# Own probabilities of two batches side by side: one 128x128 transpose for two heads, turns and weighings moved by a step

## The chip, the cores and the metric

The kernel runs on one core of a Trainium2 chip. The metric is the time of one execution on the device in microseconds (us). The engines are TensorE (PE, with its weight loads PEld), VectorE (DVE), ScalarE (ACT), GpSimd (POOL) and SyncE (SP, which only issues DMAs here). They run side by side, each in its own order, and wait for each other on semaphores.

## The reference

One decoder layer on x of shape 8 x 64 x 256 (batch, query, width) with a context of 8 x 1601 x 256, in fp32:

```python
x = x + xattn(layernorm(x), ctx, ctx)      # 16 heads of 16; keys and values from the 1601 rows of the context
x = x + attn(layernorm(x), causal=True)    # own attention: 16 heads, 64 queries x 64 keys in each batch
x = x + moe(layernorm(x))                  # 8 experts 256 -> 1024 -> 256, the best 2 by a softmax router
```

The change concerns the own attention: scores q k / 4 under a causal mask, softmax over the 64 keys, and the weighted sum of the values.

## The kernel before

The 512 tokens are four tiles of 128 rows, each two batches of 64 queries. The cross attention is the bulk: `tile(t, units)` runs 26 steps for a tile, 13 (`KT`) blocks of 128 context rows for its first batch (`bi` 0) and 13 for its second. In a step PE adds the shift and computes the scores of the block (lines 1386 and 1400), ACT takes the exponentials (line 743), POOL adds them into `prob_sum` (line 494), and PE weighs the values with them a step later (line 1220). PE begins step n only when the exponentials of step n-1 are done (line 1378); ACT begins those of step n only when POOL's sum of step n-2 is. At the second step of a batch PE computes the denominators of the batch before from `prob_sum` (line 1418 waits for POOL's last sum) and DVE then takes the heads out of the bank (lines 858 and 859).

Other work is woven into these steps as *units*, each filling one PSUM bank: K (keys of the next batch), M (a product whose row maximum DVE takes, line 927), V (values, lines 1211 and 633), X (the shift rows, lines 1260 and 637), and the *chain* of what follows the cross attention for the tile before. `CHAIN_AT` says at which step each piece of the chain runs in tiles 1 and 2, `CHAIN_AT_LAST` in tile 3, and `CHAIN_ALONE` in the tail, where the chain of the last tile runs among the first expert's products. `step_units` puts the units of a step in order (M, K, chain, V), and `Units` gives them banks in rotation: five banks (`RING_BANKS`), from the second half of tile 3 on three (`LATE_BANKS`), in the tail four (`ALONE_BANKS`). A unit waits until the unit that had its bank before has been read (`wait_free`), by ACT if its kind is in `READ_BY_ACT`, else by DVE. All instructions of an engine stand in one order written out by these tables.

The part of the chain that the change touches, in tiles 1 and 2, by step:

- 8 and 10: `s0`, `s1`, own scores of the tile's batch 0 and 1 (line 1324). DVE adds the mask (944), takes the row maxima (845) and subtracts them (846); ACT takes the exponential a step later (674); DVE sums and divides two steps later (851 to 853). The result is `soft`, 128 rows (two heads of 64 queries) by 8 pairs of heads by 64 keys, once for each batch.
- 12: `t00`, `t01`, the transposes of batch 0's probabilities, four pairs of heads in each: PE turns 128 x 64 into 64 x 128 in partitions 0 to 63 of the bank (1334). ACT copies 64 x 512 to `probs2` (652).
- 13: `t10`, `t11`, the same for batch 1 into partitions 64 to 127, as plain fp32 products with the identity (1336), which the trace shows as two passes each.
- 14 and 15: `o0`, `o1`, the values weighed (1343 to 1345); DVE takes each head's part (837, 838). At 17 follows `y2`, the output projection (1349).

In tile 3 these stand at 7, 9, 11, 12 and 14 (`o0` and `o1` together); in the tail at 5, 7 and 8.

## Time and profile before

| | before |
|---|---|
| timed runs (us) | 658.1, 660.2, 660.26; median 660.2 |
| profiled execution (us) | 658.37, its span 656.6 |
| busy: PE, PEld | 628.2 (96%), 530.1 (81%) |
| busy: DVE, ACT, POOL | 472.9 (72%), 329.8 (50%), 305.1 (46%) |
| mean granted clock of TensorE | 0.995 |
| L1334, transposes of batch 0 | 32 of 272 ns |
| L1336, passes for batch 1 | 64 of 275 ns |
| L652, copies to `probs2` | 16 of 590 ns |

The span runs from the first to the last instruction; 1.8 us of the execution lie around it. Busy times of PE overlap: matmuls are pipelined, and what one costs is the distance to the start of the next, not its duration. The main loop's tile 1 runs from about 141 us, tile 2 from about 250, tile 3 from about 359, and the experts' work with the tail's chain begins at about 445.

### The profile page before, as it was taken

The numbers are of one execution on the slowest core, as the hardware profiler recorded it, in microseconds if no ns is written. First come the engines' busy times: TensorE is split into PE (matmuls) and PEld (weight loads), VectorE is DVE, ScalarE is ACT, GpSimd is POOL, SyncE is SP. The second block draws the span as 40 slices with busy tenths as digits, with TensorE's granted clock in tenths as the row PEclk, the third lists the DMA queues.
The fourth block names the chain that finished last, engine by engine and source line by source line (L and its number), as shares of the span: only waits on it lengthen the run. The fifth ranks groups of instructions, "written<-read, shape, count | busy, mean of one in ns | idle before, by whom it ended". The sixth has DMA issues, their size and how long they took to land.

```text
span 656.6 us, 15592 instructions
## 1 busy us (share of the span) xinstructions
PE 628.2 (96%) x6312; PEld 530.1 (81%) x6312; DVE 472.9 (72%) x878; ACT 329.8 (50%) x541; POOL 305.1 (46%) x386
## 2 busy tenths in 40 slices
PE   6989999999989999998999999988989999999997
PEld 4778878868877877887887887767889999999997
DVE  4887767757697687587876867587777667756653
ACT  4355655555555564546465546474554444444421
POOL 2138788898696798687779868200000000000000
PEclk9999999999999999999999999999979999999999
DMA  6312011010010010011100000333003311330000
GB/s 183 137 46 57 27 51 27 27 51 27 27 38 15 27 52 26 26 27 51 27 27 26 2 1 2 128 132 129 1 4 125 129 50 80 128 128 0 0 0 33
DMA packets 13285, 34.11 MB, mean 52 GB/s; under 512 B 1563, under 2 KB 10532, under 8 KB 11044
## 3 DMA queue, kind: packets, MB, share of 16 engines
q1 hardware_dynamic: 13188, 33.19, 15.2%
q8 instruction: 46, 0.75, 0.5%
q14 instruction: 19, 0.16, 0.1%
q0 software_dynamic: 32, 0.01, 0.0%
HBM read 32.67 MB, written 0.52 MB: 51 GB/s over the span
## 4 chain that ended last, share of the span: by engine, by line
PE 69%; DVE 14%; POOL 8%; issue 5%; ACT 2%; DMA 1%; SPq 0%; POOLq 0%; DVEq 0%; ACTq 0%
PE bank L1211 44%; POOL prob_sum L494 8%; PE bank L1400 7%; PE bank L1220 6%; PE bank L1386 3%; PE bank L1281 3%; DVE maxes L927 2%; DVE prob_sum L494 2%; DVE ctx_lo L478 1%; DVE k_lo L908 1%; PE bank L1336 1%; DVE shift L869 1%; ACT k_hi L630 1%; PE bank L1308 1%; DVE qbd L873 1%
## 5 line engine op out<-in xcount | busy, mean ns | idle before, releaser
L494 POOL TENSOR_TENSOR prob_sum<-probs,prob_sum 128x256 f32<-128x256 f32 x336 | 273.9, 846 | 61.6 <-ACT probs L743 56.1
L743 ACT ACTIVATE probs<-bank 128x1024 f32<-128x1024 f32 (+1 forms) x104 | 106.7, 1026 | 110.1 <-PE bank L1400 80.9
L927 DVE TENSOR_REDUCE maxes<-bank 128x1 f32<-128x400 f32 (+1 forms) x256 | 129.4, 564 | 16.5 <-PE bank L1281 16.0
L725 ACT ACTIVATE h_raw<-bank,b_sb 128x512 f32<-128x512 f32 (+2 forms) x72 | 46.2, 642 | 104.9 <-PE bank L1211 101.0
L908 DVE SCALAR_TENSOR_TENSOR k_lo<-bank,bias_sb,k_hi 128x400 fp32r<-128x400 f32 (+2 forms) x64 | 40.4, 631 | 47.6 <-ACT k_hi L630 47.5
L1211 PE MATMUL bank<-w_hi,h_hi 128*128 128x256 f32 x256 | 73.7, 288 | 0.5 <-DVE h_lo L1146 0.5
L1211 PE MATMUL bank<-w_lo,h_hi 128*128 128x256 f32 x256 | 73.1, 286 | 0.0
L1211 PE MATMUL bank<-w_hi,h_lo 128*128 128x256 f32 x256 | 73.1, 285 | 0.0
L1220 PE MATMUL bank<-probs,v_sb 128*32 128x128 f32 (+1 forms) x1664 | 67.0, 279 | 2.0 <-ACT probs L743 1.9
L1145 DVE CAST h_hi<-h_raw 128x512 fp32r<-128x512 f32 (+2 forms) x72 | 28.5, 396 | 55.9 <-ACT h_raw L725 54.5
L1211 PE MATMUL bank<-wv_hi,ctx_hi 128*128 128x256 f32 (+1 forms) x208 | 65.1, 313 | 2.8 <-DVE maxes L927 2.6
L1400 PE MATMUL bank<-qbd_hi,k_hi 64*128 64x256 f32 (+1 forms) x416 | 66.5, 314 | 0.0
L1281 PE MATMUL bank<-k_hi,qbd_hi 64*128 64x400 f32 (+1 forms) x256 | 58.6, 443 | 1.0 <-DVE qbd_hi L885 0.4
L1400 PE MATMUL bank<-qbd_lo,k_hi 64*128 64x256 f32 (+1 forms) x416 | 58.8, 277 | 0.0
L1400 PE MATMUL bank<-qbd_hi,k_lo 64*128 64x256 f32 (+1 forms) x416 | 58.7, 277 | 0.0
L1211 PE MATMUL bank<-wv_lo,ctx_hi 128*128 128x256 f32 (+1 forms) x208 | 58.4, 281 | 0.0
L1211 PE MATMUL bank<-wv_hi,ctx_lo 128*128 128x256 f32 (+1 forms) x208 | 58.1, 279 | 0.0
L633 ACT ACTIVATE v_sb<-bank 128x256 f32<-128x256 f32 (+1 forms) x104 | 39.8, 382 | 35.5 <-PE bank L1211 32.0
L630 ACT ACTIVATE k_hi<-bank,bias_sb 128x400 fp32r<-128x400 f32 (+2 forms) x64 | 38.1, 596 | 38.2 <-PE bank L1211 38.2
L1211 PE MATMUL bank<-xn_hi,w_hi 128*128 128x512 f32 (+2 forms) x144 | 55.1, 382 | 0.0
L1211 PE MATMUL bank<-xn_hi,w_lo 128*128 128x512 f32 (+2 forms) x144 | 54.4, 377 | 0.0
L1211 PE MATMUL bank<-xn_lo,w_hi 128*128 128x512 f32 (+2 forms) x144 | 54.3, 377 | 0.0
(155 smaller groups left out, 1386.7 us busy)
## 6 DMA issues: line engine op xcount, KB each, us to landing
raw<-in_w SPq DMA_DIRECT2D x16, 1024.0 KB, 6.8
ctx_raw<-in_ctx_t SPq DMA_DIRECT2D x16, 400.0 KB, 3.6
ctx_raw<-in_ctx_t SPq DMA_DIRECT2D x8, 402.0 KB, 3.7
ctx_raw<-in_ctx_t SPq DMA_DIRECT2D x8, 399.0 KB, 3.6
w_sb<-in_w_t SPq DMA_DIRECT2D x1, 1280.0 KB
w_raw<-in_w_t SPq DMA_DIRECT2D x2, 256.0 KB, 4.7
result<-x_all SPq DMA_DIRECT2D x4, 128.0 KB, 1.9
x_all<-in_x SPq DMA_DIRECT2D x1, 384.0 KB, 4.1
```

Source lines behind the costliest of these rows:

```text
L494: ins = engine.tensor_tensor(prob_sum[0:ROWS[k], cols], probs[0:ROWS[k], s % 2, cols], acc[0:ROWS[k]], ALU.add)
L630: nc.scalar.activation(k_hi[parity][:, g, EDGE[c]:EDGE[c + 1]], src[:, EDGE[c] - CH[c]:CW], ACT.Identity, bias=bias_sb[:, 1, g:g + 1]).the ...
L633: nc.scalar.activation(v_sb[0:ROWS[u], u * D:u * D + D], src[0:ROWS[u], 0:D], ACT.Copy).then_inc(read_act, 1)
L725: nc.scalar.activation(h_raw[:, c % 2, 0:width], bank[:, at, 0:width], ACT.Gelu, bias=b1_sb[:, bass.ds(e, 1), c:c + 1].rearrange("p a b -> ...
L743: nc.scalar.activation(probs[0:ROWS[k], s % 2, :].rearrange("p (g n) -> p g n", g=G), bank[0:ROWS[k], score_bank(b, k):score_bank(b, k) + ...
L908: nc.vector.scalar_tensor_tensor(out=k_lo[parity][:, g, EDGE[c]:EDGE[c + 1]], in0=src[:, EDGE[c] - CH[c]:CW], scalar=bias_sb[:, 1, g:g + 1 ...
L927: nc.vector.tensor_reduce(maxes[:, g * PAIRS + j, c:c + 1], src[:, 0:width], AX.X, ALU.max).then_inc(read_dve, 1)
L1145: link(nc.vector.tensor_copy(h_hi[:, c % 4, 0:width], h_raw[:, c % 2, 0:width]))
L1211: last = nc.tensor.matmul(dst, lhs, rhs, start=(start and n == 1), stop=(stop and n == 3 * len(pairs)), **more)
L1220: ins = nc.tensor.matmul(dst_bank[32 * j:32 * j + 32, (at + g) * P:(at + g + 1) * P], lhs(g, j), p_rows[:, m * P:(m + 1) * P], start=(star ...
L1281: ins = nc.tensor.matmul(dst[:, 0:width], qbd_hi[rows, parity, g, 2 * i:2 * i + 2, :].rearrange("p s q -> p (s q)"), k_hi[parity][rows, g, ...
L1400: ins = nc.tensor.matmul(bank[0:rows, score_bank(b, k) + r, g * RH * Q:(g + 1) * RH * Q], stays, moves, start=False, stop=(part == 2), ski ...
```

## The change

`soft` is laid out with the two batches of a pair of heads side by side, so that one transpose of 128 x 128 turns both: query rows of two heads by 64 keys of batch 0 and 64 keys of batch 1. Four units `t00`, `t01`, `t10`, `t11` become two, `t0` and `t1`, which wait for the division of both batches; the products with the identity are gone. The copies to `probs2` take all 128 partitions. In tiles 1 and 2 the turns stand at step 14 and both weighings at 15; in tile 3 the turns at 13 and the weighings at 14 as before; in the tail the places stay. With two units fewer the banks rotate otherwise, and in the tail `gt` and `b2` get banks by name. DVE and ACT reach a batch's part of `soft` in pieces of 64 with a step of 128.

```diff
--- before.py
+++ after.py
@@ -100,15 +100,15 @@
 OWN_V = {0: 11, 1: 12}
 LAST_V_AT = 1
 
-CHAIN_AT = {3: ["y1"], 5: ["xt1"], 6: ["qk", "v"], 8: ["s0"], 10: ["s1"], 12: ["t00", "t01"], 13: ["t10", "t11"],
-            14: ["o0"], 15: ["o1"], 17: ["y2"], 19: ["xt2"], 20: ["router"], 24: ["gt"], 25: ["b2"]}
-
-CHAIN_AT_LAST = {2: ["y1"], 4: ["xt1"], 5: ["qk", "v"], 7: ["s0"], 9: ["s1"], 11: ["t00", "t01"],
-                 12: ["t10", "t11"], 14: ["o0", "o1"], 16: ["y2"], 18: ["xt2"], 19: ["router"], 23: ["gt"],
-                 24: ["b2"]}
-CHAIN_ALONE = {1: ["y1"], 2: ["xt1"], 3: ["qk"], 5: ["s0", "s1", "v"], 7: ["t00", "t01", "t10", "t11"],
+CHAIN_AT = {3: ["y1"], 5: ["xt1"], 6: ["qk", "v"], 8: ["s0"], 10: ["s1"], 14: ["t0", "t1"],
+            15: ["o0", "o1"], 17: ["y2"], 19: ["xt2"], 20: ["router"], 24: ["gt"], 25: ["b2"]}
+
+CHAIN_AT_LAST = {2: ["y1"], 4: ["xt1"], 5: ["qk", "v"], 7: ["s0"], 9: ["s1"], 13: ["t0", "t1"], 14: ["o0", "o1"],
+                 16: ["y2"], 18: ["xt2"], 19: ["router"], 23: ["gt"], 24: ["b2"]}
+CHAIN_ALONE = {1: ["y1"], 2: ["xt1"], 3: ["qk"], 5: ["s0", "s1", "v"], 7: ["t0", "t1"],
                8: ["o0", "o1"], 9: ["y2"], 11: ["xt2"], 12: ["router"], 15: ["gt"], 16: ["b2"]}
 ALONE_BANKS = [6, 2, 7, 3]
+GATE_BANKS = {"gt": 3, "b2": 6}
 DONE_TILES = TT - 1
 FIRST_HIDDEN = {0: [2], 1: [3], 3: [4], 6: [5], 7: [6], 9: [7]}
 FIRST_GELU = {0: [0, 1], 1: [2], 2: [3], 4: [4], 8: [5, 6], 9: [7]}
@@ -126,7 +126,7 @@
     return [("M", ROW_TILES * u + r) for u in pairs for r in range(ROW_TILES)]
 
 
-READ_BY_ACT = {"p1", "p2", "p3", "v", "V", "VL", "X", "xt1", "qk", "t00", "t01", "t10", "t11", "xt2", "router", "gt"}
+READ_BY_ACT = {"p1", "p2", "p3", "v", "V", "VL", "X", "xt1", "qk", "t0", "t1", "xt2", "router", "gt"}
 
 
 class Units:
@@ -153,6 +153,9 @@
         self.early = sum(len(self.at[s]) for s in range(KT))
         self.bank = [late_banks[n % len(late_banks)] if late_banks and n >= self.early else banks[n % len(banks)]
                      for n in range(len(order))]
+        if banks is ALONE_BANKS:
+            for n, kind in enumerate(order):
+                self.bank[n] = GATE_BANKS.get(kind, self.bank[n])
 
     def counts(self, n):
 
@@ -330,7 +333,7 @@
         own = masked[:, 0:2 * G, :]
         odd = masked[:, 2 * G:4 * G, :]
         neg_max2 = sb("neg_max2", [P, 2, G * PAIRS])
-        soft = sb("soft", [P, 2, G * PAIRS, Q])
+        soft = sb("soft", [P, G * PAIRS, 2, Q])
         row_sums2 = sb("row_sums2", [P, 2, G * PAIRS])
         odd2 = sb("odd2", [P, 2, G, Q])
         probs2 = sb("probs2", [P, G * 512])
@@ -647,10 +650,8 @@
                 elif kind == "v":
                     nc.scalar.activation(v2[:, :], src[:, 0:D], ACT.Copy).then_inc(read_act, 1)
                 elif kind[0] == "t":
-                    bi, g = int(kind[1]), int(kind[2])
-                    rows = slice(bi * Q, bi * Q + Q)
-                    nc.scalar.activation(probs2[rows, g * 512:g * 512 + 512], src[rows, :], ACT.Copy)\
-                        .then_inc(read_act, 1)
+                    g = int(kind[1])
+                    nc.scalar.activation(probs2[:, g * 512:g * 512 + 512], src, ACT.Copy).then_inc(read_act, 1)
                 elif kind == "xt2":
                     nc.scalar.activation(xn_t[:, :, :].rearrange("p c n -> p (c n)"), src[:, 0:D],
                                          ACT.Copy).then_inc(read_act, 1)
@@ -671,7 +672,7 @@
                     if kind in ("s0", "s1"):
                         bi = int(kind[1])
                         act.wait_ge(soft_ready, 2 * t + bi + 1)
-                        nc.scalar.activation(soft[:, bi], soft[:, bi], ACT.Exp).then_inc(soft_exp_done, 1)
+                        nc.scalar.activation(soft[:, :, bi, :], soft[:, :, bi, :], ACT.Exp).then_inc(soft_exp_done, 1)
 
             def step(units, s, t, b, parity):
 
@@ -842,15 +843,15 @@
                 return values.unsqueeze(2).broadcast_to([P, G * PAIRS, Q])
 
             def subtract_maxima(bi):
-                link(nc.vector.tensor_reduce(neg_max2[:, bi], soft[:, bi], AX.X, ALU.max, negate=True))
-                nc.vector.tensor_tensor(soft[:, bi], soft[:, bi], by_row(neg_max2[:, bi]), ALU.add).then_inc(soft_ready, 1)
+                link(nc.vector.tensor_reduce(neg_max2[:, bi], soft[:, :, bi, :], AX.X, ALU.max, negate=True))
+                nc.vector.tensor_tensor(soft[:, :, bi, :], soft[:, :, bi, :], by_row(neg_max2[:, bi]), ALU.add).then_inc(soft_ready, 1)
 
             def divide_rows(bi, count):
 
                 dve.wait_ge(soft_exp_done, count)
-                link(nc.vector.tensor_reduce(row_sums2[:, bi], soft[:, bi], AX.X, ALU.add))
+                link(nc.vector.tensor_reduce(row_sums2[:, bi], soft[:, :, bi, :], AX.X, ALU.add))
                 link(nc.vector.reciprocal(row_sums2[:, bi], row_sums2[:, bi]))
-                nc.vector.tensor_tensor(soft[:, bi], soft[:, bi], by_row(row_sums2[:, bi]), ALU.mult).then_inc(rows2_ready, 1)
+                nc.vector.tensor_tensor(soft[:, :, bi, :], soft[:, :, bi, :], by_row(row_sums2[:, bi]), ALU.mult).then_inc(rows2_ready, 1)
 
             def own_heads(src, read, count):
 
@@ -941,7 +942,7 @@
                                             ALU.add).then_inc(read_dve, 1)
                 elif kind in ("s0", "s1"):
 
-                    nc.vector.tensor_tensor(soft[:, int(kind[1])], src.rearrange("p (n k) -> p n k", k=Q),
+                    nc.vector.tensor_tensor(soft[:, :, int(kind[1]), :], src.rearrange("p (n k) -> p n k", k=Q),
                                             causal_sb[:, :].unsqueeze(1).broadcast_to([P, G * PAIRS, Q]),
                                             ALU.add).then_inc(read_dve, 1)
                 elif kind in ("o0", "o1"):
@@ -1326,19 +1327,16 @@
                                                    k2_t[:, g, bi * Q:bi * Q + Q], start=True, stop=True)
                 elif kind[0] == "t":
 
-                    bi, g = int(kind[1]), int(kind[2])
-                    pe.wait_ge(rows2_ready, 2 * t + bi + 1)
+                    g = int(kind[1])
+                    pe.wait_ge(rows2_ready, 2 * t + 2)
                     for j in range(PAIRS):
-                        turned, own_rows = dst[bi * Q:bi * Q + Q, j * P:j * P + P], soft[:, bi, g * PAIRS + j, :]
-                        if bi == 0:
-                            ins = nc.tensor.transpose(turned, own_rows, ident[:, :])
-                        else:
-                            ins = nc.tensor.matmul(turned, own_rows, ident[:, :], start=True, stop=True)
+                        ins = nc.tensor.transpose(dst[:, j * P:j * P + P],
+                                                  soft[:, g * PAIRS + j].rearrange("p b q -> p (b q)"), ident[:, :])
                 elif kind in ("o0", "o1"):
 
                     bi = int(kind[1])
                     rows = slice(bi * Q, bi * Q + Q)
-                    units.wait_read_act(pe, read_act, f"t{bi}1")
+                    units.wait_read_act(pe, read_act, "t1")
 
                     nc.tensor.matmul(dst[:, 0:E], ones_bf[:, :], ident_bf[:, 0:E], start=True, stop=True)
                     ins = weigh_heads(dst, 0, lambda g, j: v2[rows, g * P + 32 * j:g * P + 32 * j + 32],
```

## Rows read from the trace of the kernel before

**Rows 1.** The page's chain that ended last: share of the span by engine
```profile
PE 69%; DVE 14%; POOL 8%; issue 5%; ACT 2%; DMA 1%; SPq 0%; POOLq 0%; DVEq 0%; ACTq 0%
```

**Rows 2.** Timeline of PE, step 12 of tile 1: start us, duration us, instruction, idle before
```profile
191.35 1.03 PE L1334 MATMUL bank<-ident,soft 128*64 128x128 f32 x8 [1.72 <-DVE soft L853]
192.14 0.36 PE L1211 MATMUL bank<-wv_hi,ctx_hi 128*128 128x256 f32 x1
...
193.59 0.39 PE L1386 MATMUL bank<-shift_rows,ones_bf 64*128 64x512 bf16 x2
```

**Rows 3.** Timeline of ACT in the same stretch
```profile
190.71 1.06 ACT L637 ACTIVATE shift_rows<-bank 128x512 bf16<-128x512 f32 x2
191.67 1.02 ACT L743 ACTIVATE probs<-bank 65x1024 f32<-65x1024 f32 x1
192.57 1.07 ACT L652 ACTIVATE probs<-bank 64x512 f32<-64x512 f32 x2
```

**Rows 4.** Timeline of PE, step 13 of tile 1
```profile
195.91 1.96 PE L1336 MATMUL bank<-ident,soft 128*64 128x128 f32 x16
197.80 0.38 PE L1211 MATMUL bank<-wv_hi,ctx_hi 128*128 128x256 f32 x1
```

**Rows 5.** Timeline of PE, steps 14 and 15 of tile 1: denominators, o0, o1
```profile
200.48 0.64 PE L1220 MATMUL bank<-prob_sum,ones_f 128*32 128x128 f32 x16
...
202.87 0.18 PE L1343 MATMUL bank<-ident_bf,ones_bf 128*128 128x8 bf16 x1
...
207.59 0.18 PE L1343 MATMUL bank<-ident_bf,ones_bf 128*128 128x8 bf16 x1
...
208.27 0.65 PE L1220 MATMUL bank<-probs,v_sb 128*32 128x128 f32 x16
```

**Rows 6.** Timeline of POOL: a sum of tile 1, two sums of tile 3
```profile
192.76 4.58 POOL L494 TENSOR_TENSOR prob_sum<-probs,prob_sum 65x256 f32<-65x256 f32 x4 [0.27 <-ACT probs L743]
...
402.89 6.45 POOL L494 TENSOR_TENSOR prob_sum<-probs,prob_sum 128x256 f32<-128x256 f32 x8 [0.76 <-ACT probs L743]
```

**Rows 7.** Timeline of DVE, step 14 of tile 1
```profile
202.23 2.03 DVE L927 TENSOR_REDUCE maxes<-bank 128x1 f32<-128x402 f32 x4
```

**Rows 8.** Timeline of PE, step 11 of tile 3
```profile
403.96 0.28 PE L1400 MATMUL bank<-qbd_hi,k_lo 64*128 64x256 f32 x2
...
405.80 0.36 PE L1211 MATMUL bank<-wv_hi,ctx_hi 128*128 128x256 f32 x1
```

**Rows 9.** Transposes: ns min/median/max by line, and one pair in PE's timeline
```profile
L1235 PEld LDWEIGHTS bank<-ident,xn x24: 138/140/143, 5.1 to 477.8; 128*128 128x128 f32 x24
L1235 PE MATMUL bank<-ident,xn x24: 271/273/329, 5.2 to 477.9; 128*128 128x128 f32 x24
...
L1334 PEld LDWEIGHTS bank<-ident,soft x32: 108/111/113, 191.3 to 467.4; 128*64 128x64 f32 x32
...
477.74 0.41 PE L1235 MATMUL bank<-ident,xn 128*128 128x128 f32 x2 [0.81 <-DVE xn L830]
```

**Rows 10.** Instructions by line and form: busy us, mean ns | idle before
```profile
L944 DVE TENSOR_TENSOR soft<-bank,causal_sb 128x512 f32<-128x512 f32 x8 | 5.5, 683 | 1.1 <-PE bank L1324 1.0
...
L859 DVE SCALAR_TENSOR_TENSOR masked<-bank,mask_sb,masked 128x256 f32<-128x256 f32 x8 | 3.9, 484 | 0.3
...
L838 DVE SCALAR_TENSOR_TENSOR o_t<-bank,mask_sb,odd 128x128 f32<-128x128 f32 x8 | 2.8, 351 | 0.3
```

**Rows 11.** Timeline of PE in the tail
```profile
468.29 1.93 PE L1336 MATMUL bank<-ident,soft 128*64 128x128 f32 x16 [0.52 <-DVE soft L853]
470.15 0.44 PE L1211 MATMUL bank<-xn_hi,w_hi 128*128 128x384 f32 x1
```

**Rows 12.** Busy time by stretch; the number after POOL's is the granted clock
```profile
478.00:482.00 4.00, 2.94 (x15) 2.70 (x14) 2.95 (x8) 2.29 (x5) 0.00 (x0) 0.64 0.01 2
482.00:486.00 4.00, 4.00 (x22) 4.00 (x20) 1.86 (x9) 1.82 (x5) 0.00 (x0) 0.51 0.00 0
486.00:490.00 4.00, 3.91 (x31) 3.41 (x31) 3.68 (x12) 3.11 (x9) 0.00 (x0) 1.00 0.00 0
```

## The prediction

> **What bounds the kernel now.** I read the chain that ended last first, because it says which engine's time is the kernel's time: 69% of it is TensorE (PE), 14% VectorE (DVE), 8% GpSimd (POOL), 2% ScalarE (ACT) [rows 1]. An instruction taken from PE is therefore worth its time, provided that PE does not meet a wait a moment later that it used to reach late. So the second view is the timeline of PE around every place where the change works. These are four: the chain of own attention runs once for each of four pairs of batches. It is woven into tiles 1, 2 and 3 of the main loop (schedules MIDDLE, MIDDLE, LAST) and once into the first expert's work (TAIL). The steps of tiles 1 and 2 repeat each other within 0.1 us in start-to-start time, so I show tile 1 and count it twice. The third view is the other engines in the same stretches, to see what is late next.
>
> **What the change removes on PE.** Per pair of batches there are now 8 transposes (batch 0, line 1334), issued in 1.03 us, and 16 matmul passes (batch 1, line 1336: 8 fp32 products of two passes each) in 1.96 us [rows 2, 4]. PE's next work starts 0.79 us after the first group (191.35 to 192.14) and 1.89 us after the second (195.91 to 197.80); the first also has a wait of 1.72 us before it, for the division of batch 0's rows by DVE [rows 2, 4]. The change puts 8 transposes of 128 columns in their place. The trace has this very shape in the transposes of the normalised tile (line 1235), but only in pairs: two take 0.41 us, one 0.27, so the second starts 0.14 us behind the first [rows 9]. Of the 64-column ones, with the same last part of 0.27, one follows the other every (1.03 - 0.27)/7 = 0.109 us [rows 2]. Bounds: 8 x 0.109 = 0.87 us and 8 x 0.14 = 1.12 us per pair; I take 1.0, between them, since the first gap of a group tends to be the long one, and a pair has no other.
>
> **Tile 1, step 12** (the next step starts at 193.59 [rows 2]). Gone are the wait and the 8 transposes: 1.72 + 0.79 = 2.5 us of PE's time. It can't use all of it. Step 13 begins with a wait for the exponentials of step 12 (line 1378), and ACT starts these at 191.67 and ends at 192.69, because they stand in its queue behind the exponential of the own scores, a split and the two copies of the shift rows, which end at 191.77 [rows 3]. None of that is touched. PE's other work of the step (V projection and weighing, 192.14 to 193.59) then ends at about 191.1, and step 13 starts at 192.75 instead of 193.59: **0.84 us** gained, and PE now idles in front of the exponentials for 1.6 us where it idled 1.72 us for the division.
>
> **Step 13.** t10 and t11 go: from 195.91 to 197.80, **1.89 us** [rows 4]. The K unit before them and the V unit behind them follow without a wait. Next comes step 14's score work and then the denominators, which wait for POOL's sum of step 12. POOL ends that at 192.76 + 4.58 = 197.34 [rows 6]; the denominators came at 200.48 [rows 5] and will come at about 200.48 - 0.84 - 1.89 = 197.75. Covered, by 0.4 us.
>
> **Step 14.** It loses o0 (0.68 us: the equal o1 starts with line 1343 at 207.59 and the next work at 208.27) and gets t0 and t1 (1.0 us): **+0.3 us** [rows 5]. Before, o0 waited for the bank that DVE's first maximum frees (DVE reads the four from 202.23 on, 0.51 us each [rows 7]); t0 takes over that wait, t1 needs the second maximum at 203.25 and the V unit the third at 203.76, each just when the transposes end. Nothing is added within 0.1 us. The new wait for both batches' rows is over before: in step 13 PE took up batch 1's rows at 195.91 with no wait [rows 4], so nothing queued behind it on PE (t0, t1, the V unit, the next weighing) is held up. In the tail the same wait ends at 468.29 as now; behind it stands the hidden product, which stood there before. **Step 15** gets o0 beside o1: **+0.68**. DVE's reads of o0 move with it, in the same number.
>
> Sum of a middle tile: -0.84 - 1.89 + 0.3 + 0.68 = -1.75; twice, **-3.5 us**. ACT gets two copies of 128x512 for four of 64x512: two of the old ones take 1.07, two copies of a whole 128x512 (the shift rows) 1.06 [rows 3], so it saves 1.07 per pair, which hides behind PE and counts nothing. DVE, ACT's exponential and PE now see `soft` in pieces of 64 with a step of 128. DVE reads of PSUM with such steps: 0.351 us for 128 elements, 0.484 for 256, so 0.133 per 128 and 0.75 for 512, against 0.683 of the present contiguous form [rows 10]. Bounds: 0 and 0.07 per instruction. In the middle tiles at most three of them lie before the exponentials of step 12 (0.2 us); in the tail ten in a row (0.7 us). I take nothing, because 0.484 is no more than the 128-element form plus its elements (two pieces or four cost the same), and keep 1.3 us for the range.
>
> **Tile 3 (LAST).** t00 and t01 stand in step 11: PE's score work starts its last pair at 403.96 and the V unit at 405.80 [rows 8]; without them it starts about 0.2 later than the last score, at 404.2: -1.6. The exponential behind it waits for PE here, not PE for it. Step 12 loses t10 and t11, -1.9 (the same 16 passes as in tile 1 [rows 4]). Step 13 gets t0 and t1, +1.0. o0 stays in step 14. Sum **-2.5 us**; POOL's sums of steps 10 and 11 ended together at 402.89 + 6.45 = 409.34 [rows 6]; step 13's exponentials wait for the second and would now be ready at about 409.8, so this cover too is 0.4 us.
>
> **Tail.** PE waits for batch 1's division until 468.29, turns its rows, and goes on to the next hidden product at 470.15 [rows 11]. The 8 transposes of batch 0, earlier, lie in a hole and count nothing; after the division come now 1.0 us instead of 1.86: **-0.85 us**. What follows (weighings, projection, normalisation, routing) is a chain of latencies and moves up as a whole.
>
> **The sum**: 3.5 + 2.5 + 0.85 = 6.85, say 6.8 us. The profiled execution took 658.4 us (span 656.6 and 1.8 around it), so it would be 651.6. The timed runs stand at 658.1, 660.2 and 660.3: two levels 2 us apart, and the profiled one belongs to the lower. The median by the upper level would be 653.4. I have no reason to expect that the levels vanish, nor which the median will catch, and forecast **652.8**, slightly nearer the upper one since that holds the median now.
>
> On the price of the transposes a rule speaks against the change. The row: a load of 64 columns for a transpose takes 0.110 us and one of 128 columns 0.140, while transposes follow each other at 0.11 and 0.14 us [rows 2, 9]. The Trainium skill, TensorE: Matmul & The Clock Gate, section LDWEIGHTS (loading the stationary operand), says that a load takes time in proportion to its columns, P/1.2 ns. By that page, as an estimate, the 24 loads of 64 columns cost 1.28 us now and the 8 of 128 columns 0.85, and the change would be worth 0.4 us per pair where I count 1.7 to 1.9; the trace's two load times don't double.
>
> **Rivals.**
> 1. *A full-width transpose costs two half-width ones.* Then 8 of them take 8 x 0.22 = 1.75 us, 0.75 more in each of the four places: 3.0 less gain, 655.8. Against it stands the pair at 0.14. Chance 0.06.
> 2. *The wait moves instead of going.* The cover of the denominators in step 14 is 0.4 us. Should POOL's sum end later, or DVE's reads take the place, the 1.89 of step 13 in two tiles is lost: gain 3.1, 657.1 by the upper level, 655.3 by the lower. For it: POOL takes 1.15 us for each of this sum's four pieces and 0.81 for one in tile 3 [rows 6], so its time is not fixed. Against: it starts at the end of the exponentials, which the change leaves. Chance 0.08.
> 3. *The clock.* TensorE's granted clock falls in the tail: 0.64 in 478 to 482 and 0.51 in 482 to 486, which is its 1.2 GHz level, after a stretch in which PE waited much, and is back to 1.00 (2.4 GHz) in 486 to 490. At the low level PE passes 22 matmuls in 4 us, at the high one 31 [rows 12], so the 6.8 us at the low level (the shares below 1.00, doubled) cost 6.8 x 9/31 = 2.0 us. That is also the distance of the two levels of the runs. The tail gets emptier, all of it before 470, so one fall may become longer or two: +2.0, 654.8 to 655.4. Chance 0.12. It may also not fall: 650.8, inside the forecast's range, chance 0.05.
> 4. *Slower than before.* The same mechanism in more places: if the new hole in front of step 12's exponentials brought the clock down in both middle tiles, and the tail had two falls more, each at 2.0 us, the time would be 652.8 + 8.0 = 660.8; with rival 2's loss, 664.5. Falls decide from four on (6.8/2.0 = 3.4), or from two beside rival 2. Against it: the present hole there is as long (1.72 us) and the transposes behind it go at full pace [rows 2]. Chance 0.03.
>
> That the change doesn't do what it says has no way open: the transposes' shape is fixed in the code.
>
> **How the numbers follow.** Forecast 0.66 (and 0.05 for the clock that doesn't fall), with its own range 650.3 to 655.2 (bounds of the transposes -0.5 and +0.5, of the steps +1.3, of the two levels -1.2 and +0.6, of chaining in the steps 0.5). Rival 1 and 3 reach to 655.8, rival 2 to 657.1. For 8 in 10 the range is 649.8 to 656.2. A change is told from none at 0.5%, 3.3 us: faster means under 656.9. Forecast, rival 1, nearly all of 3 and most of 2 lie there; faster 0.87, same 0.09, slower 0.04.
>
> **What would show it.** In the profile after: 32 transposes of 128 columns issued 0.11 to 0.14 apart, no line 1336; step 12 of tiles 1 and 2 shorter by 0.8 with PE waiting for the exponentials (ACT line 743) instead of for line 853; step 13 shorter by 1.9, step 14 longer by 0.3, step 15 by 0.7; the last matmul of the main loop 6.0 us earlier and the tail 0.85 shorter; eight copies of 128x512 on ACT in place of sixteen. It would be wrong if POOL's sum or DVE's reads are what ends PE's wait in step 14, if the steps from 16 on give back the gain (POOL-bound steps at the end of a tile), or if low-clock stretches are more or longer than the one now.

## The result, and the profile after

| | before | changed |
|---|---|---|
| median of the runs made together (4 and 4), us | 660.23 | 650.94 |
| lowest to highest, us | 658.1 to 660.71 | 649.42 to 654.02 |
| ratio of the times, 95% interval | | 0.9879 [0.9853, 0.9905] |
| profiled execution and its span, us | 658.37, 656.6 | 654.02, 652.1 |
| its mean granted clock | 0.995 | 0.990 |

The change makes the kernel 1.2% faster. The forecast was 652.8 with a range of 649.8 to 656.2. In 20 runs of the changed kernel over this study the median is 651.4, in 52 of the kernel before 658.9: 7.5 us apart. (The ratios given here and below are not the quotients of the medians beside them; the two differ by up to 0.003.) One warning before the profile is read: the profiled execution of the changed kernel is the slowest of its four, and its clock is the lowest (0.990; the others had 0.993, 0.994 and 0.996). Two later profiles of the same kernel are used to tell what belongs to the kernel and what to that one execution.

The line numbers moved by one to three: the transposes are L1333 (before L1334 and L1336), their copies L654 (L652), the scores' exponentials L744 (L743), the denominators and weighings L1221 (L1220), POOL's sums L497 (L494), the division L854 (L853), the shift rows' products L1384 (L1386).

First the page's busy times and its chain of what ended last.

```profile
PE 624.3 (96%) x6240; PEld 527.0 (81%) x6248; DVE 472.4 (72%) x878; ACT 324.3 (50%) x533; POOL 304.9 (47%) x386
PE 71%; DVE 10%; POOL 9%; issue 5%; ACT 3%; DMA 0%; POOLq 0%; DVEq 0%; ACTq 0%
```

PE is still the bound, and by 71% instead of 69% [rows 1]; DVE's share fell from 14 to 10%. Now the timeline of PE through steps 12 to 14 of tile 1 (start us, duration us, instruction, idle before it and what ended that).

```profile
191.05 0.64 PE L1221 MATMUL bank<-probs,v_sb 128*32 128x128 f32 x16
193.32 0.39 PE L1384 MATMUL bank<-shift_rows,ones_bf 64*128 64x512 bf16 x2 [1.62 <-ACT probs L744]
...
195.38 0.35 PE L1212 MATMUL bank<-ctx_hi,wk_lo 128*128 128x402 f32 x1
195.56 0.28 PE L1212 MATMUL bank<-wv_hi,ctx_hi 128*128 128x256 f32 x1
...
196.95 0.39 PE L1384 MATMUL bank<-shift_rows,ones_bf 64*128 64x512 bf16 x2
198.16 0.65 PE L1221 MATMUL bank<-prob_sum,ones_f 128*32 128x128 f32 x16
...
200.54 1.14 PE L1333 MATMUL bank<-ident,soft 128*128 128x128 f32 x8
201.51 0.33 PE L1212 MATMUL bank<-wv_hi,ctx_hi 128*65 128x256 f32 x1
...
202.94 0.39 PE L1384 MATMUL bank<-shift_rows,ones_bf 64*128 64x512 bf16 x2
```

Read it against [rows 2, 4, 5]. The wait of 1.72 us for the division and the transposes behind it are gone from step 12; in their place PE waits 1.62 us for the exponentials. In step 13 the last K product (195.38) is followed by the V unit 0.18 us later; before, the 16 passes for batch 1 stood there, and the next work came 1.89 us after their start. In step 14 the eight full-width transposes keep PE for 0.97 us (200.54 to 201.51). The denominators at 198.16 have no wait in front. The next two lines are ACT, the third POOL, in the same stretch:

```profile
191.30 1.06 ACT L640 ACTIVATE shift_rows<-bank 128x512 bf16<-128x512 f32 x2
192.25 1.01 ACT L744 ACTIVATE probs<-bank 65x1024 f32<-65x1024 f32 x1
193.34 4.62 POOL L497 TENSOR_TENSOR prob_sum<-probs,prob_sum 65x256 f32<-65x256 f32 x4 [0.26 <-ACT probs L744]
```

The order of ACT is that of [rows 3], with the exponentials right behind the shift rows. POOL's sum ends at 193.34 + 4.62 = 197.96, and PE asks for it at 198.16: 0.20 us of cover, where the kernel before had 3.1.

**Where the time came from.** A step's length is the distance from its first shift-row product to the next step's. The table gives lengths before minus lengths after, in us; the steps not named differ by 0.03 or less and add up to 0.1 to 0.2, which the main loop's row includes (but for tile 3's step 24 in profile 1, where the clock fell: below).

| stretch | forecast | profile 1 | profile 3 |
|---|---|---|---|
| tile 1: step 12, 13, 14, 15 | 0.84, 1.89, -0.3, -0.68 | 0.85, 2.05, -0.29, -0.69 | 0.86, 2.05, -0.29, -0.69 |
| tile 2, the same | the same | 0.87, 2.06, -0.29, -0.71 | 0.86, 2.06, -0.29, -0.70 |
| tile 3: step 11, 12, 13 | 1.6, 1.9, -1.0 | 1.62, 1.89, -0.82 | 1.62, 1.90, -0.83 |
| main loop together | 6.0 | 6.7 | 6.6 |
| tail, the turn after the division | 0.85 | 1.05 | 1.05 |
| together | 6.85 | 7.8 | 7.65 |

In the tail PE's lines show the last term against [rows 11]: from the transposes to the next hidden product it was 470.15 - 468.29 = 1.86 us and is 0.81.

```profile
464.65 1.06 PE L1333 MATMUL bank<-ident,soft 128*128 128x128 f32 x8 [1.61 <-DVE soft L854]
465.46 0.42 PE L1212 MATMUL bank<-xn_hi,w_hi 128*128 128x384 f32 x1
```

**What took some of it back in profile 1.** 7.8 us are gained and the span is only 656.6 - 652.1 = 4.5 shorter. The prologue ended 0.7 us later in this execution than in the kernel before (in the two other profiles of the changed kernel within 0.02: that is the execution and not the kernel). The rest is the clock. Busy time of PE, PEld, DVE, ACT and POOL by stretch; the number after POOL's is the granted clock:

```profile
432.00:436.00 4.00, 3.48 (x40) 2.34 (x44) 3.94 (x5) 3.71 (x7) 0.00 (x0) 0.71 0.00 0
436.00:440.00 4.00, 4.00 (x48) 2.67 (x41) 2.82 (x5) 1.92 (x3) 0.00 (x0) 0.50 0.00 0
440.00:444.00 4.00, 4.00 (x46) 3.11 (x45) 2.11 (x3) 2.66 (x5) 0.00 (x0) 0.94 0.45 152
...
472.00:476.00 4.00, 1.94 (x11) 1.46 (x10) 2.63 (x9) 1.03 (x3) 0.42 (x1) 0.83 0.00 0
476.00:480.00 4.00, 4.00 (x20) 4.00 (x20) 3.01 (x11) 2.90 (x5) 0.00 (x0) 0.50 0.01 2
480.00:484.00 4.00, 3.91 (x25) 3.41 (x25) 2.40 (x8) 2.69 (x7) 0.00 (x0) 0.82 0.00 0
```

The fall in the tail is the one of [rows 12]. The fall to the 1.2 GHz level from about 434 to 440 is not in the profile of before. (POOL stands at 0.00 in the first rows because in these last steps DVE adds the exponentials.) Counted from the start of the span, which leaves in the 0.7 of the prologue, PE was 6.0 us ahead of before at the start of step 24 and 3.64 at the denominators of the last batch, so this fall cost about 2.4 us. 7.8 - 0.7 - 2.4 = 4.7, against 4.5 measured.

### The profile page after: what moved, and what is told of

It is laid out like the page before. It is cut to its first block, busy times and chain, and to the rows that moved or that the text cites. A ratio compares the mean times of both kernels' runs of the same rounds, so it can differ in the third digit from the quotient of the medians.

```text
span 652.1 us, 15440 instructions
## 1 busy us (share of the span) xinstructions
PE 624.3 (96%) x6240; PEld 527.0 (81%) x6248; DVE 472.4 (72%) x878; ACT 324.3 (50%) x533; POOL 304.9 (47%) x386
## 4 chain that ended last, share of the span: by engine, by line
PE 71%; DVE 10%; POOL 9%; issue 5%; ACT 3%; DMA 0%; POOLq 0%; DVEq 0%; ACTq 0%
PE bank L1212 45%; POOL prob_sum L497 9%; PE bank L1398 7%; PE bank L1221 7%; PE bank L1384 3%; PE bank L1282 3%; DVE maxes L928 2%; ACT probs L744 1%; DVE ctx_lo L481 1%; DVE prob_sum L497 1%; DVE k_lo L909 1%; ACT k_hi L633 1%; PE bank L1309 1%; DVE qbd L874 1%; DVE soft L847 1%
## 5 line engine op out<-in xcount | busy, mean ns | idle before, releaser
L497 POOL TENSOR_TENSOR prob_sum<-probs,prob_sum 128x256 f32<-128x256 f32 x336 | 273.8, 845 | 63.1 <-ACT probs L744 57.4
L744 ACT ACTIVATE probs<-bank 128x1024 f32<-128x1024 f32 (+1 forms) x104 | 106.6, 1025 | 113.4 <-PE bank L1398 88.4
L1221 PE MATMUL bank<-probs,v_sb 128*32 128x128 f32 (+1 forms) x1664 | 67.9, 281 | 2.0 <-ACT probs L744 1.9
```

What stands on the lines that cost most here:

```text
L497: ins = engine.tensor_tensor(prob_sum[0:ROWS[k], cols], probs[0:ROWS[k], s % 2, cols], acc[0:ROWS[k]], ALU.add)
L744: nc.scalar.activation(probs[0:ROWS[k], s % 2, :].rearrange("p (g n) -> p g n", g=G), bank[0:ROWS[k], score_bank(b, k):score_bank(b, k) + ...
L1221: ins = nc.tensor.matmul(dst_bank[32 * j:32 * j + 32, (at + g) * P:(at + g + 1) * P], lhs(g, j), p_rows[:, m * P:(m + 1) * P], start=(star ...
```

## Experiments

The theory: all the gain is instructions taken off PE (8 full-width transposes in place of 8 half-width ones and 16 passes), and the division's wait goes because the exponentials' wait behind it covers it; where the turns stand is of little weight; the rest of the time is clock falls. The rivals: the gain comes from the move (turns and weighings a step later, out of the division's way) and the merging adds little; a full-width transpose has a price that eats some of it; the move itself creates the fall. Each experiment's times stand beside 14 to 17 runs of the kernel before on the same chip.

### Merging alone

```diff
-CHAIN_AT = {..., 10: ["s1"], 14: ["t0", "t1"], 15: ["o0", "o1"], 17: ...}
+CHAIN_AT = {..., 10: ["s1"], 13: ["t0", "t1"], 14: ["o0"], 15: ["o1"], 17: ...}
-CHAIN_AT_LAST = {..., 9: ["s1"], 13: ["t0", "t1"], 14: ["o0", "o1"], ...}
+CHAIN_AT_LAST = {..., 9: ["s1"], 12: ["t0", "t1"], 14: ["o0", "o1"], ...}
```

> The changed kernel with the new turns at the old places: t0, t1 at step 13 with o0 at 14 and o1 at 15 in tiles 1 and 2, t0, t1 at step 12 of tile 3. Theory A (the gain is the PE time of the removed instructions and the hole in front of the batch-0 division; the move by a step is worth nothing by itself): step 12 shorter than before by 0.85 us, step 13 by 1.05 (2.05 less 1.0 for the turns), steps 14 and 15 as before; sum -1.9 per middle tile, the same as the changed kernel's 1.93; tile 3 -2.5; whole main loop within 0.2 us of the changed kernel. Rival B (the move is needed, since both divisions must be done): PE waits in step 13 for the second division (line 854), which ends at about 193.6 against PE's 195.6, so B would show a wait there and give 1 to 2 us back per tile.

Measured: 649.75 us (3 runs, 649.65 to 650.77), ratio 0.9865 [0.9816, 0.9914]. Tile 1's step 12 is 0.87 shorter than before and step 13 1.19; tile 3's steps 11 and 12 are 1.62 and 1.06 shorter; steps 14 and 15 are as before. The main loop gains 6.8 us, the changed kernel 6.6 to 6.7. PE's timeline in step 13:

```profile
192.60 0.39 PE L1384 MATMUL bank<-shift_rows,ones_bf 64*128 64x512 bf16 x2 [1.60 <-ACT probs L744]
...
194.66 0.35 PE L1212 MATMUL bank<-ctx_hi,wk_lo 128*128 128x402 f32 x1
194.84 1.04 PE L1333 MATMUL bank<-ident,soft 128*128 128x128 f32 x8
195.63 0.36 PE L1212 MATMUL bank<-wv_hi,ctx_hi 128*128 128x256 f32 x1
```

The turns start with no wait for DVE, although they are a step earlier than in the change, and PE goes on 0.79 us after their start. So the whole gain is there without the move. The profile of this kernel has the fall behind step 24 too, though its turns and weighings stand at the old steps, so the move is not what makes it (the last number but two is the clock):

```profile
432.00:436.00 4.00, 4.00 (x44) 2.65 (x36) 3.94 (x6) 3.38 (x6) 0.00 (x0) 0.51 0.00 0
```

### Moving alone

```diff
-CHAIN_AT = {..., 12: ["t00", "t01"], 13: ["t10", "t11"], 14: ["o0"], 15: ["o1"], ...}
+CHAIN_AT = {..., 14: ["t00", "t01", "t10", "t11"], 15: ["o0", "o1"], ...}
-CHAIN_AT_LAST = {..., 11: ["t00", "t01"], 12: ["t10", "t11"], 14: ["o0", "o1"], ...}
+CHAIN_AT_LAST = {..., 13: ["t00", "t01", "t10", "t11"], 14: ["o0", "o1"], ...}
```

(In the kernel before.)

> The kernel before with its four units t00, t01, t10, t11 moved together to step 14 (tile 3: step 13) and o0 and o1 to 15 (tile 3: 14), its 8 transposes and 16 passes kept. Theory A: step 12 -0.85, step 13 -2.05, step 14 +2.1 (24 instructions, 2.75 us, for o0's 0.68), step 15 +0.7: about -0.1 per middle tile; tile 3 -1.6 -1.9 +2.8 = -0.7; tail unchanged; main loop shorter by 0.9 us in all, total 1 us or less. Rival B (the schedule makes the gain): most of the main loop's 6.7 us remain.

Measured: 658.33 us (9 runs), ratio 0.9990 [0.9962, 1.0019]: no difference that the runs can tell. The steps show why it comes to nothing: step 12 0.84 shorter, step 13 2.07 shorter, step 14 2.26 longer, step 15 0.67 longer. Up to step 20 of tile 3 the main loop gains 0.67 us, where 0.9 was expected.

```profile
199.96 1.11 PE L1334 MATMUL bank<-ident,soft 128*64 128x128 f32 x8
201.00 1.96 PE L1336 MATMUL bank<-ident,soft 128*64 128x128 f32 x16
202.89 0.33 PE L1211 MATMUL bank<-wv_hi,ctx_hi 128*65 128x256 f32 x1
```

The work that left steps 12 and 13 stands whole in step 14: 2.93 us from 199.96 to 202.89. So merging is the change's gain; the move is an exchange between steps. That the move took the division's wait away is true (step 12 is 0.84 shorter), but merging alone does that as well. The 0.67 us are lost again in steps 21 and 22 of tile 3 (0.45 and 0.31 longer): ACT waits there for a transfer of the expert's weights, and the exponentials behind it come late. One profile shows it; whether every execution has it no other run tells.

```profile
428.35 0.63 ACT L717 ACTIVATE w_hi<-raw 128x512 fp32r<-128x512 f32 x1 [0.66 <-DMA raw<-in_w]
```

### The price of a full-width transpose

```diff
                     for j in range(PAIRS):
-                        ins = nc.tensor.transpose(dst[:, j * P:j * P + P], ...)
+                        for _ in range(2):
+                            ins = nc.tensor.transpose(dst[:, j * P:j * P + P], ...)
```

> The changed kernel with each of its 8 transposes per pair of batches done twice in a row (same result). Measures what one 128x128 transpose costs in place. Theory A (0.12 us each, no more than half-width ones, which follow each other at 0.109): against the changed kernel step 14 of tiles 1 and 2 longer by 0.95, step 13 of tile 3 by 0.95, the tail by 0.95: 3.8 in all. Rival H (a full-width transpose costs its load time twice over, 0.19 to 0.22): 1.5 to 1.75 in each place, 6 to 7 in all.

Measured: 654.87 us (8 runs), ratio 0.9929 [0.9891, 0.9966]. Step 14 is 0.78 us longer than in the changed kernel, tile 3's step 13 by 0.88 and the tail by 0.88, where 0.95 was expected, so eight more transposes cost 0.10 to 0.11 us each.

```profile
200.26 1.97 PE L1334 MATMUL bank<-ident,soft 128*128 128x128 f32 x16
201.98 0.36 PE L1212 MATMUL bank<-wv_hi,ctx_hi 128*65 128x256 f32 x1
```

Sixteen in 1.72 us, 0.107 each: the same distance as that of the 64-column ones, 0.109 [rows 2]. The load of 128 columns takes longer than that of the 64-column transposes (0.14 against 0.11 us), but the issue doesn't follow it. Nor does the load's time follow the columns: the passes of before load 64 columns in 0.137. The view by line of the changed kernel, and the passes' loads in the kernel before:

```profile
L1333 PEld LDWEIGHTS bank<-ident,soft x32: 138/140/144, 200.5 to 465.3; 128*128 128x128 f32 x32
L1333 PE MATMUL bank<-ident,soft x32: 272/273/329, 200.5 to 465.4; 128*128 128x128 f32 x32
...
L1336 PEld LDWEIGHTS bank<-ident,soft 128*64 128x64 f32 x64 | 6.9, 137 | 1.5 <-issue 1.3 <-ACT shift_rows L637 0.2
```

### The holes filled

```diff
+            def fill(dst, count):
+                for _ in range(count):
+                    nc.tensor.matmul(dst, ones_bf[:, :], ones_bf[:, :].unsqueeze(1).broadcast_to([P, 4, P]),
+                                     start=True, stop=True)
...
                 units.wait_free(pe, read_act, read_dve, n)
+                if units is LAST and kind == "gt":
+                    fill(dst, 7)
+                if units is TAIL:
+                    fill(dst, {"y1": 5, "t0": 7, "y2": 4, "xt2": 3, "router": 2}.get(kind, 0))
```

The products go into the unit's own bank, which the unit then overwrites.

> The changed kernel with useless bf16 products of 512 columns (0.22 us each) in the holes where PE waits: 7 before the gate's transpose at step 23 of tile 3, and in the tail 5 before y1, 7 before t0, 4 before y2, 3 before xt2, 2 before the router. They write the unit's own bank before the unit does. Theory C: the clock stays at 1.00, both falls of the profiled run of the changed kernel go (at 433.6 and at 475), mean clock 1.00, and the time is 4.5 us under the profiled run and at or 1 to 2 us under the median of the changed kernel, about 649, with less spread. Rival E (what an engine waits for, not the clock, sets these stretches; the products are on the path): the clock changes or not, but the time stays, or rises by up to 2 us where a product runs past its hole.

Measured: 649.72 us (6 runs), ratio 0.9882 [0.9829, 0.9936], in two groups: 649.06 to 649.95 at a clock of 0.996 to 0.999, and 658.05 and 658.10 at 0.984. The profile is of the second group:

```profile
472.00:476.00 4.00, 3.16 (x20) 3.07 (x21) 3.49 (x12) 2.73 (x4) 0.00 (x0) 0.82 0.02 6
476.00:480.00 4.00, 4.00 (x22) 4.00 (x21) 2.92 (x11) 2.32 (x7) 0.00 (x0) 0.50 0.00 0
...
484.00:488.00 4.00, 4.00 (x21) 4.00 (x20) 1.82 (x6) 1.12 (x3) 0.00 (x0) 0.50 0.40 117
...
492.00:496.00 4.00, 4.00 (x14) 3.23 (x14) 0.89 (x3) 1.21 (x2) 0.00 (x0) 0.62 0.00 0
```

The fall at 434 is gone, that in the tail isn't, against the expectation: it came although PE was busy for 3.16 of the 4 us in which it began, and it stayed for some 20 us while PE was busy without a break. Filling the tail didn't protect it here.

### One hole filled

The same, with the `TAIL` lines left out: seven products in front of `gt` in tile 3 alone.

> The changed kernel with 7 useless bf16 products before the gate's transpose at step 23 of tile 3 only; nothing in the tail. Theory C: the fall of the clock at about 433 doesn't come (it cost 1.1 to 2.4 us in three profiles of kernels without the filling), the fall at about 475 stays; mean clocks 0.995 to 0.997 in most runs instead of 0.993 to 0.995, median about 649.6 against 651.1. Rival I (the clock falls with the same chance anywhere, filled or not): mean clocks as in the changed kernel, median 651.

Measured: 649.98 us (6 runs, 649.59 to 650.14), ratio 0.9856 [0.9815, 0.9897], all six at a clock of 0.996 or 0.997. PE's timeline of the changed kernel, then of this one, at the end of step 23:

```profile
430.37 0.27 PE L1359 MATMUL bank<-ident,gate_tile 128*8 128x128 f32 x1
432.52 0.65 PE L1221 MATMUL bank<-probs,v_sb 128*32 128x128 f32 x16 [1.88 <-ACT probs L744]
```
```profile
429.92 1.68 PE L1250 MATMUL bank<-ones_bf 128*128 128x512 bf16 x7
431.44 0.27 PE L1367 MATMUL bank<-ident,gate_tile 128*8 128x128 f32 x1
432.07 0.65 PE L1221 MATMUL bank<-probs,v_sb 128*32 128x128 f32 x16 [0.36 <-ACT probs L744]
```

And the stretches of this one:

```profile
428.00:432.00 4.00, 3.62 (x42) 1.95 (x40) 3.85 (x9) 1.77 (x4) 0.00 (x0) 1.00 0.01 4
432.00:436.00 4.00, 3.63 (x60) 2.62 (x62) 3.94 (x5) 3.71 (x7) 0.00 (x0) 1.00 0.00 0
```

What is left of the wait of 1.88 us is 0.36; the useless products in it cost nothing (steps 23 and 24 are as long as before), and the clock stays at 1.00. Of the 17 runs of the three unfilled variants timed on the same chip (the doubled transposes and the two kernels below) 8 have a clock under 0.995, of this one's six none. Of the nine profiles of kernels that leave the hole open, four show the fall (the changed kernel's first and second, merging alone, moving alone) and five don't. That ties the hole to the fall, by few runs; the kernel under "Both together" adds five.

### The sum's cover taken away

```diff
-CHAIN_AT = {..., 8: ["s0"], 10: ["s1"], 14: ["t0", "t1"], ...}
+CHAIN_AT = {..., 8: ["s0"], 9: ["s1"], 14: ["t0", "t1"], ...}
```

This takes the exponential of `s1` out from in front of the cross attention's in step 12: if ACT's order is what holds step 12, the step gets shorter, and POOL, which has 0.2 us to spare, should be next.

> The changed kernel with s1 at step 9 of tiles 1 and 2 instead of 10, so that DVE's softmax of batch 1 and ACT's exponential of it come a step earlier and no longer stand before the exponentials of step 12, for which PE idles 1.6 us. Theory F (POOL is late next: its sums run without a pause from 179 to 192.4 and the denominators wait for the sum of step 12): step 12 shorter by 1.3 to 1.5 than in the changed kernel, but the denominators of step 14 come only 0.3 to 0.6 us earlier, PE waiting about 1 us for POOL; 0.5 per tile, 1 us in all. Rival G (only ACT's queue is late): 1.4 per tile stay, 2.8 us in all.

Measured: 651.12 us (3 runs), ratio 0.9875 [0.9821, 0.9929]. Steps of tile 1 against before: step 9 2.67 longer, step 10 1.97 shorter, 12 2.53 shorter, 13 1.87 shorter, 14 1.60 longer, 15 0.69 longer. A middle tile gains 1.4 where the changed kernel gains 1.9. Neither theory had this: both saw a gain over the changed kernel, by 0.5 or 1.4 a tile. Step 12 does what was expected and more (1.68 shorter than in the changed kernel, 1.3 to 1.5 expected); what wasn't counted is that steps 9 and 10 together get 0.69 longer, with PE idle for 0.84 us in front of the moved scores (line 1325, at 180.81), and that the denominators wait. The three lines are PE, POOL and ACT:

```profile
198.42 0.65 PE L1221 MATMUL bank<-prob_sum,ones_f 128*32 128x128 f32 x16 [0.82 <-POOL prob_sum L497]
186.28 12.09 POOL L497 TENSOR_TENSOR prob_sum<-probs,prob_sum 128x256 f32<-128x256 f32 x12 [1.58 <-ACT probs L744]
194.82 1.03 ACT L744 ACTIVATE probs<-bank 128x1024 f32<-128x1024 f32 x1 [2.52 <-POOL prob_sum L497]
```

POOL runs twelve pieces from 186.28 without a break and ends at 198.37, and the denominators wait 0.82 us for it, the exponentials of the next block 2.52. This is the second rival of the prediction, made real: the wait goes to POOL once PE's lead is more than the 0.2 us of cover.

### The same, with the turns in the hole

The last edit on top of the first one (`s1` at 9, turns at 13, in tile 3 at 12, weighings at 14 and 15).

> The kernel of e6 with the turns at step 13 and o0, o1 at 14 and 15 as in the merged kernel that isn't moved (tile 3: turns at 12). Theory F: in steps 12 and 13 PE has about 1 us of idle time in front of the denominators, which the turns now fill: 0.9 to 1.0 us per middle tile less than e6, main loop 2.5 to 3 us shorter than the changed kernel, about 648 at its clock. Rival G (no wait for POOL, PE alone bounds): equal to e6 within 0.1 us, as the places made no difference in the changed kernel.

Measured: 649.94 us (6 runs, 647.61 to 652.46), ratio 0.9857 [0.9810, 0.9904]. Steps 12, 13 and 14 are 2.53 and 1.19 shorter and 0.62 longer than before, the main loop gains 7.8 us, 1.1 more than the changed kernel (2.5 to 3 more were expected; against the kernel above it is 1.0 a tile, as expected).

```profile
194.43 1.03 PE L1333 MATMUL bank<-ident,soft 128*128 128x128 f32 x8
198.51 0.65 PE L1221 MATMUL bank<-prob_sum,ones_f 128*32 128x128 f32 x16 [0.21 <-POOL prob_sum L497]
```

Here the place of the turns does matter: at 13 they stand in time that PE would otherwise spend waiting for POOL. The wait in front of the denominators is 0.21 us where it was 0.82. The lowest two runs, 647.61 and 647.70, have a clock of 0.999; the highest two, 652.25 and 652.46, one of 0.990.

### Both together

The last kernel with the seven products of the one-hole kernel in front of `gt`.

> The kernel of e9 (s1 at 9, turns at 13, tile 3's at 12) with the 7 useless products of e8 before the gate's transpose at step 23 of tile 3. If the two effects add (theories C and F): main loop 1.1 us shorter than the changed kernel's and no fall of the clock at about 433; mean clocks 0.996 to 0.999, median about 648.5, against the changed kernel's 651.1. If the fall only moves elsewhere (rival I): mean clocks 0.990 to 0.995 and 650.

Measured: 649.04 us (5 runs, 648.15 to 650.68; about 648.5 was expected), ratio 0.9854 [0.9826, 0.9882]. The profile has no fall in tile 3, the main loop gains 7.6 us, and all five clocks are 0.995 or more, where on the same chip 7 of 9 runs of the changed kernel are under that. It is the version that beats both kernels: its median is 2.5 us below the changed kernel's 651.51 on that chip, four of its five runs lie below the lowest of the other's nine (649.77), and its interval against the kernel before ends at 0.9882, where the other's [0.9883, 0.9944] begins. Its own two edits account for it, as far as these runs go: 0.9 to 1.0 us in the loop, and the fall behind step 24.

### The changed kernel again, twice

> The changed kernel once more, for more pairs of time and mean granted clock. Theory C (what differs between runs is how many low-clock stretches fall in the holes of tile 3's last steps and of the tail, 2.0 to 2.4 us each): times lie near 647.4, 649.4 to 651 and 653 to 654, each 2.4 us with the mean clock 0.003 to 0.004 lower; every step outside these stretches equal within 0.05 us. Rival D (other noise): no such relation, differences spread over all steps.

Measured: 651.12 us (7 runs, 649.94 to 660.15), ratio 0.9882 [0.9844, 0.9919]. No run stands at the 647.4 expected of an execution without these falls, and the profiled one, at 660.15 and a clock of 0.979, lies above all the levels that were expected.

> The changed kernel on the same chip beside e10, for a direct comparison. Theory C: median 651, mean clocks 0.992 to 0.995 in most runs, with the fall at about 433 in the profile; steps equal to those of the first profile within 0.05 us. Rival D: other places.

Measured: 651.51 us (9 runs, 649.77 to 658.61), ratio 0.9913 [0.9883, 0.9944]. Outside the falls the steps are those of the first profile within 0.05 us in both. The clock is not. The third profile (span 647.9) has the same hole in front of step 24 (1.90 us), no fall behind it, and a shorter one in the tail:

```profile
430.00:434.00 4.00, 1.80 (x32) 1.35 (x31) 4.00 (x5) 2.93 (x5) 0.00 (x0) 1.00 0.00 0
472.00:476.00 4.00, 3.28 (x16) 3.28 (x17) 3.43 (x12) 3.13 (x5) 0.00 (x0) 0.57 0.01 2
```

So the kernel alone doesn't fix the fall; executions of one kernel differ in it. The sum of the third profile: 6.6 (loop) + 1.05 (tail) = 7.65, and PE's last product comes 8.75 us earlier than before, so the shorter fall gave 1.1; the spans are 656.6 - 647.9 = 8.7 apart.

The runs of the two kernels by their mean granted clock (us; the 48 of before whose clock is known and the 20 of the changed one):

| clock | before | changed |
|---|---|---|
| 0.999 | 656.2 to 657.1 | none |
| 0.995 to 0.997 | 656.8 to 659.2 | 649.4 to 651.1 |
| 0.992 to 0.994 | 659.8 to 661.4 | 650.9 to 652.2 |
| 0.989 to 0.991 | 660.1 to 661.0 | 653.9 to 654.0 |
| 0.979 to 0.984 | 665.1 to 668.3 | 658.6 to 660.2 |

At one clock the kernels lie about 8 us apart: the median of the 17 runs of before at 0.996 and 0.997 is 658.1, that of the four of the changed kernel at 0.996 is 649.8. Two clocks 0.01 apart differ by some 6 us within a kernel: from 656.6 at 0.999 to 668.3 at 0.979 is 11.7 for 0.020.

## Why the prediction was right, and where it was off

**What bounds the kernel.** Right: what is taken from PE is taken from the time. All eight terms came within 0.2 us, and no step from 16 on gave anything back.

**Step 12 (0.84).** Right, 0.85 and 0.87, and for the reason given: ACT's queue. The wait for the exponentials is 1.62 us where 1.6 was forecast. The kernel with `s1` at 9 shows it by intervention: with one exponential less in front of them the same step is 2.53 shorter.

**Step 13 (1.89).** Short by 0.16. The distance from the start of the passes to the next work was the wrong stretch to take away: the gap from the last K product to the passes (195.63 to 195.91, 0.28 us) became 0.18 to the V unit, which is 0.10 of it. The rest is in the V unit itself: its second product starts 0.22 us behind its first when the passes stand before it (197.80 to 198.02) and 0.12 when the K product does (195.56 to 195.68), and the unit as a whole gained 0.09; the K side lost 0.02. A group's cost is the distance between its two neighbours, with and without it.

**Step 14 (-0.3) and 15 (-0.68).** Right, -0.29 and -0.69: the transposes in the step take 0.97 where 1.0 stood.

**The price of the transposes (1.0 for eight; bounds 0.87 and 1.12).** Right in step 14 only, where the first gap is 0.165 and t1 starts 0.154 behind t0's last. Elsewhere the eight take 0.79 (merging alone, step 13), 0.81 (tail) and 0.85 (tile 3), which is below my lower bound. Inside a group they follow each other at 0.109 in every place; the first gap is 0.11 to 0.17. The row I rested on was one pair, 0.14 apart [rows 9]; the twelve pairs of that line are 0.11 to 0.17 apart. I said that a pair has only the first gap and still let it pull the estimate up. That is the term that was mis-sized: by 0.2 in tile 3 and in the tail each. It also answers the rule I had set against the row. The Trainium skill, TensorE: Matmul & The Clock Gate, section LDWEIGHTS (loading the stationary operand), prices a load by its columns. Here the transposes' load grows from 0.110 to 0.140 us for twice the columns, far from double, and the passes' load of 64 columns takes 0.137; the distance between transposes doesn't grow: 0.109 us at 64 and at 128 columns. The trace decides: what was paid was the number of instructions.

**Tile 3 (2.5) and tail (0.85).** 2.69 and 1.05. The first two terms were exact (1.62 and 1.89); the rest is again the price of the transposes.

**Strides (0, up to 1.3).** Zero was right. DVE and ACT took the same time for pieces of 64 with a step of 128 as for the contiguous rows: the mask 684 ns against 683 [rows 10].

```profile
L945 DVE TENSOR_TENSOR soft<-bank,causal_sb 128x512 f32<-128x512 f32 x8 | 5.5, 684 | 1.1 <-PE bank L1325 1.0
L654 ACT ACTIVATE probs<-bank 128x512 f32<-128x512 f32 x8 | 4.3, 597 | 2.0 <-PE bank L1333 1.8
```

The second line is the copies: 8 of 128x512 at 597 ns in place of 16 of 64x512 at 590, so half of ACT's copy time went, beside PE as said.

**The rivals.** The first (a full-width transpose costs double) is refuted by the doubled transposes: 0.10 to 0.11 us for one more. The second (the wait moves) did not happen, but with less room than I gave it: 0.20 us of cover instead of 0.4, because PE gained 0.16 more in step 13 than I had counted. The kernel with `s1` at 9 shows it: there the wait has moved to POOL. The third (one fall more) is half right. It happened, in the profiled execution among others, at 2.4 us where 2.0 was forecast, but not in the tail where I looked, and not because of the change: the hole of 1.88 us in front of step 24 is in the kernel before as well, behind the gate's transpose at 436.4, and its profile has no fall there. The profile of the moved-alone kernel, whose work is that of before, shows both falls at a clock of 0.992 and 660.10 us:

```profile
436.00:440.00 4.00, 2.10 (x33) 1.39 (x31) 4.00 (x6) 2.17 (x3) 0.00 (x0) 0.89 0.00 0
440.00:444.00 4.00, 4.00 (x35) 2.51 (x34) 3.94 (x7) 2.61 (x5) 0.00 (x0) 0.50 0.02 4
...
484.00:488.00 4.00, 4.00 (x27) 4.00 (x26) 2.35 (x11) 2.65 (x7) 0.00 (x0) 0.64 0.00 0
```

The runs of before at 0.992 are the upper of the two levels that the prediction had seen (658.1 and 660.2) and couldn't explain; by this profile the likely explanation is the fall behind step 24, there or not there. The fourth rival (slower) found no ground.

**The total.** Forecast 652.8, measured 650.9 (651.4 over all runs). Of the 1.9 us, 0.8 to 0.9 are the terms above (7.65 to 7.8 instead of 6.85). The rest is the level: 652.8 was built on the slower level of before (660.2), minus 6.8, drawn 0.6 towards the lower, while the median of before over all its 52 runs is 658.9. Both errors point the same way, so none hid the other: with the terms as measured the forecast would have been 651.9, and with 658.9 for the level besides 651.2, against 651.4 over all runs. The changed kernel's tail fall was in one profile 1.1 us cheaper than that of before; whether it is so on average no run here settles. One sum of the forecast's own range is off: its bounds downwards (0.5, 1.2 and 0.5) lead from 652.8 to 650.6, not to 650.3.

**What stays open.** Why a fall lasts 4 us in one execution and 20 in another with PE busy all the while (the filled kernel; the second profile of the changed one, 476 to 496 at 0.50 to 0.57), and whether the changed kernel falls behind step 24 more often than the one before: 15 of its 20 runs have a clock under 0.995, of before 22 of 48, and 7 of before reach 0.999, none of it; but a mean clock doesn't tell where in the execution the falls were. In the profiles the change only shifts this hole by 6 us; no run shifts it alone. Nor was the changed kernel tried without the banks given by name to `gt` and `b2`.

## What to carry to other kernels

Small transposes and small fp32 products cost by the instruction: put two narrow ones side by side so that one full-width instruction does both, and count instructions, not columns (here 0.109 us each at 64 and at 128 columns). Before moving work between steps to escape a wait, ask whether the wait in front of the next step covers it anyway: here the move alone was worth nothing, and the merged turns gained as much in their old place. When PE gets faster, look at how much cover each partner has left (POOL: 0.2 us here); where the cover is used up, work is best placed in front of the wait, which is what made the moved scores pay (1.1 us in the loop).

## What the runs showed of the chip that was not expected

- Full-width fp32 transposes (128 columns) issue 0.109 us apart in a group, no slower than half-width ones, although their weight load takes 0.14 instead of 0.11 us; only the first gap of a group was longer, up to 0.17.
- An fp32 product with the identity took two passes of 0.12 us each (16 in 1.89), so eight products cost more than twice what eight transposes of the same shape did (0.79).
- A wait of 1.9 us on PE was followed by a fall of the granted clock to 0.50 for about 7 us in some executions and by none in others of the same kernel; with seven useless products in the wait, none of three profiled executions shows it, and the 11 runs of the two kernels that fill only this wait all have a mean clock of 0.995 or more. A fall in the tail began while PE was nearly full, and lasted 20 us while it was full.
- The mean granted clock of an execution of one kernel told its time within some 1.5 us, and 0.01 of it went with about 6 us. One run of the doubled transposes (657.69 us at 0.942) is the exception, and has no profile.
